# Queries of the third block: the bias added by products on TensorE, the constant factor moved out of the rounding chain

## What is computed

```python
def _L1_xattn_ref(x, cond, Wq, bq, Wkv, bkv, Wp, bp):
    ...
    q = (x @ Wq + bq).reshape(1, B * N, H, hd)
    ...
    scale = 1.0 / np.sqrt(hd).astype(np.float32)
    q = jnp.transpose(q * scale, (0, 2, 1, 3))
    ...
    q = _fq_sym(q, axis=-1)
    k = _fq_sym(k, axis=-1)
    ...
    attn = jnp.einsum('bhqd,bhkd->bhqk', q, k)
```

## Time and profile before

| | |
|---|---|
| median of 3 runs | 398.62 us (398.0 to 398.7) |
| span of the profiled execution | 396.3 us |
| PE busy | 301.0 us (76%) |
| DVE busy | 338.2 us (85%) |
| ACT busy | 316.7 us (80%) |
| POOL busy | 144.8 us (37%) |
| mean granted clock of PE | 0.926 |

### The profile page before, as it was taken

How to read it: one execution, slowest core, us unless ns; L and a number is a source line. 1 busy time by engine, 2 the same in 40 slices (tenths; PEclk the granted TensorE clock), 3 DMA queues, 4 the chain that set the end, 5 groups by cost and what they waited for, 6 DMA issues and landing times.

```text
span 396.3 us, 7494 instructions
## 1 busy us (share of the span) xinstructions
PE 301.0 (76%) x2589; PEld 186.2 (47%) x2589; DVE 338.2 (85%) x556; ACT 316.7 (80%) x517; POOL 144.8 (37%) x315
## 2 busy tenths in 40 slices
PE   7988999766796987567777857767576766884957
PEld 6755565322585874333444534444344343432434
DVE  4668999868889988778899998889999999678995
ACT  3785689967255789688999989899999999887771
POOL 6424524569500504004124565412222132247330
PEclk9989999899899999876899997999999999999576
DMA  8900023400200016569999988799899969800001
GB/s 268 388 5 3 0 74 96 203 2 0 106 0 2 2 29 124 107 99 173 163 168 175 177 158 132 140 185 174 151 156 166 156 130 148 136 1 2 26 31 50
DMA packets 126342, 42.68 MB, mean 108 GB/s; under 512 B 121056, under 2 KB 124768, under 8 KB 125536
## 3 DMA queue, kind: packets, MB, share of 16 engines
q1 hardware_dynamic: 125872, 41.60, 53.9%
q0 software_dynamic: 144, 0.52, 0.3%
q10 hardware_dynamic: 288, 0.07, 0.1%
HBM read 11.24 MB, written 1.05 MB: 31 GB/s over the span
## 4 chain that ended last, share of the span: by engine, by line
DVE 28%; PE 24%; ACT 23%; issue 16%; POOL 7%; DMA 1%; SPq 0%; ACTq 0%; DVEq 0%; POOLq 0%
ACT rb L973 15%; DVE nm L1452 5%; PE ps L1920 4%; PE ps L2015 4%; PE ps L1991 2%; DVE st L1108 2%; PE ps L2120 2%; PE ps L1785 1%; DVE ra L1557 1%; PE ps L2027 1%; DVE small L1559 1%; POOL ra L557 1%; POOL ra L558 1%; DMA xs<-x 1%; PE ps L1893 1%
## 5 line engine op out<-in xcount | busy, mean ns | idle before, releaser
L1452 DVE TENSOR_REDUCE nm<-ps 128x1 f32<-128x1024 f32 x128 | 153.1, 1217 | 12.6 <-PE ps L2015 11.6
L973 ACT ACTIVATE rb<-ps,eb,sq 128x1024 int16<-128x1024 f32 x128 | 153.7, 1214 | 11.8 <-POOL eb L639 11.1
L2015 PE MATMUL ps<-ra,rb 128*128 128x512 bf16 x256 | 82.8, 409 | 49.0 <-ACT rb L973 48.4
L639 POOL TENSOR_SCALAR eb<-nm,sq 128x1 f32<-128x1 f32 x128 | 34.2, 267 | 123.1 <-DVE nm L1452 122.1
L2015 PEld LDWEIGHTS ps<-ra,rb 128*128 128x128 bf16 x256 | 15.8, 99 | 67.7 <-ACT rb L973 63.9
L2042 PEld LDWEIGHTS ps<-ra,tern 128*128 128x128 f16 x624 | 26.0, 99 | 18.9 <-issue 9.2
L2042 PE MATMUL ps<-ra,tern 128*128 128x16 f16 x624 | 26.0, 171 | 2.6 <-DVE rb L1183 2.6
L973 ACT ACTIVATION_READ_ACCUMULATOR rb<-ps,eb,sq 128x1 f32 x128 | 27.0, 211 | 0.0
L1893 PE MATMUL ps<-xqT,tern 128*128 128x512 bf16 x64 | 17.2, 406 | 6.0 <-DVE rb L1361 4.9
L2027 PEld LDWEIGHTS ps<-idh,rb 128*128 128x128 f16 x224 | 14.3, 99 | 14.3 <-issue 7.7
L2027 PE MATMUL ps<-idh,rb 128*128 128x128 f16 x224 | 17.5, 222 | 4.6 <-issue 2.2
(11 more groups left out here) (240 smaller groups left out, 714.0 us busy)
## 6 DMA issues: line engine op xcount, KB each, us to landing
stage<-w SPq DMA_DIRECT2D x2, 1024.0 KB, 7.3
rb<-ra SPq DMA_DIRECT2D x16, 128.0 KB, 3.1
xs<-x SPq DMA_DIRECT2D x4, 256.0 KB, 4.5
cx<-ctx_in SPq DMA_DIRECT2D x4, 256.0 KB, 4.7
stage<-w_gate SPq DMA_DIRECT2D x1, 1024.0 KB, 7.7
stage<-w_up SPq DMA_DIRECT2D x1, 1024.0 KB, 10.6
stage<-w_down SPq DMA_DIRECT2D x1, 1024.0 KB, 4.8
cx<-wide_rows SPq DMA_DIRECT2D x1, 1024.0 KB, 7.9
```

What stands on the lines that cost most here:

```text
L639: nc.gpsimd.tensor_scalar(eb[:, u % 3:u % 3 + 1], nm[:, u % 3:u % 3 + 1], sq[:, t, h:h + 1], LN255, ALU.mult, ALU.add).then_inc(s_bias, 1)
L973: A(esc[u % E_RING], bank(2 * (u % 3), 2), ACT.Exp, bias=eb[:, u % 3:u % 3 + 1], scale=sq[:, t, h:h + 1], accum_out=es[:, t % 2, h:h + 1]) ...
L1452: V.tensor_reduce(nm[:, u % 3:u % 3 + 1], bank(2 * (u % 3), 2), AX.X, ALU.max, negate=True).then_inc(s_max, 1)
L2015: ins = M(bank(2 * (u % 3) + hf), qz[t % 2][:, h // 2, h % 2, :], kT[:, h // 2, 512 * hf:512 * hf + 512], start=True, stop=True)
```

## The change

The bias of the queries is added by a product on PE: `ones` (one row of 128) by `bq` (one row of 256) starts each sum in PSUM, and the two products of the projection add to it. DVE reads the sums from PSUM twice and writes no copy. The scale is made in two steps: `ks`, without the factor, from which the reciprocal is taken, and `sq`, which is `ks` times the factor; nothing on DVE waits for `sq`. The lower limit is divided by the factor.

```diff
-            def quantise_rows(psum, bias, factor, scale, out_i):
-
-
-                link(V.tensor_tensor(kb.rearrange("p (b n) -> p b n", b=2), psum.rearrange("p (b n) -> p b n", b=2),
-                                     bias.unsqueeze(1).to_broadcast([P, 2, D]), ALU.add))
-                kb3 = kb.rearrange("p (a d) -> p a d", d=HD)
-                link(V.tensor_reduce(ka[:, :], kb3, AX.X, ALU.max, apply_absolute_value=True))
-                link(V.tensor_scalar(scale, ka[:, :], factor / 127.0, QMIN, ALU.mult, ALU.max))
-                link(V.reciprocal(kr[:, :], scale))
-                if factor != 1.0:
-                    link(V.tensor_scalar(kr[:, :], kr[:, :], factor, None, ALU.mult))
-                return V.tensor_tensor(out_i.rearrange("p (a d) -> p a d", d=HD), kb3,
+            def quantise_rows(psum, factor, scale, out_i):
+
+
+                rows3 = psum.rearrange("p (a d) -> p a d", d=HD)
+                link(V.tensor_reduce(ka[:, :], rows3, AX.X, ALU.max, apply_absolute_value=True))
+                link(V.tensor_scalar(ks[:, :], ka[:, :], 1.0 / 127.0, QMIN / factor, ALU.mult, ALU.max))
+                V.tensor_scalar(scale, ks[:, :], factor, None, ALU.mult)
+                link(V.reciprocal(kr[:, :], ks[:, :]))
+                return V.tensor_tensor(out_i.rearrange("p (a d) -> p a d", d=HD), rows3,
                                        kr[:, :].unsqueeze(2).to_broadcast([P, 2 * H, HD]), ALU.mult)
...
-                quantise_rows(bank(Q_BANK), rowv["bq"], 0.25, sq[:, 2 * j:2 * j + 2, :].rearrange("p t h -> p (t h)"),
+                quantise_rows(bank(Q_BANK), 0.25, sq[:, 2 * j:2 * j + 2, :].rearrange("p t h -> p (t h)"),
                               ki).then_inc(q_int, 1)
...
                 for i in range(2):
                     t = 2 * j + i
+                    M(bank(Q_BANK)[:, D * i:D * i + D], ones[0:1, :], rowv["bq"][0:1, :], start=True, stop=False)
                     for k in range(2):
                         ins = M(bank(Q_BANK)[:, D * i:D * i + D], xn3T[:, k, P * t:P * t + P], wqs[:, k, :],
-                                start=(k == 0), stop=(k == 1))
+                                start=False, stop=(k == 1))
                 ins.then_inc(q_ps, 1)
```

## The result

| | median | runs | profiled execution: span, mean granted clock |
|---|---|---|---|
| before | 398.31 us | 397.97 to 398.7, 4 | 396.3 us, 0.926 |
| changed | 407.9 us | 405.86 to 409.27, 4 | 405.8 us, 0.870 |

The ratio is 1.0204, with a 95% interval of 1.0165 to 1.0244: slower, by some four times what was forecast (400.7 against 398.62 us, 0.5%). Medians are over all runs; ratios and intervals leave out runs more than 1.5% above the fastest of the same kernel, so a ratio can differ from that of the two medians. Two later comparisons of the same two programs gave 1.0139 (1.0093 to 1.0185) and 1.0179 (1.0120 to 1.0238).

The account below looks back on a forecast made before the run. No one engine bounds the whole; locally a PE and DVE chain does. Delay of +1.75 us after pairs 0 and 1 becomes +1.85, then +2.1: 396.3 + 2.1 = 398.4, plus 2.3 outside the span, 400.7 us; range 398.3 to 403.5.

Parts of the forecast that it names:

- What bounds: Third block's queries, 134 to 174 us: no one engine bounds; PE and DVE steps follow one another, late pairs without slack.
- DVE gives 0.8 us a pair: q_quant4 on DVE: bias add and factor multiplication leave the chain, saving 0.65 to 0.83 us a pair, 0.8 taken.
- dearer reading from PSUM: q_quant4 on DVE: by the skill's page two PSUM reads cost 0.13 us a pair, saving 0.67 instead of 0.8.
- PE pays 1.53 us a pair at full clock: Each q_project on PE: two one-row bias products lengthen it from 1.74 to 3.27 us, as in k_project.
- rival of the cheap bias: Each q_project: a bias product costs like any other, 0.87 us a projection instead of 1.53; 399.1 us, chance 0.08.
- Pairs 0 and 1, +1.75 us: First two query pairs: PE's delay less DVE's savings makes q_quant4(1) end and scores(4) start 1.75 us later.
- Pairs 2 and 3 cost almost nothing more: q_project(2) and (3): later starts move work out of the slow stretch; +1.85 after pair 2, +2.1 at attend(0).
- rival of the lasting low clock: q_project(2) and (3) wholly at 0.50, 6.4 us each: +4.15, then +2.5, together +6.7; 405.3 us, chance 0.10.
- The starting time: Whole kernel before the change: span 396.3 us, median of the runs 398.62 us, the 2.3 us between carried over.

Follow-up runs that it names:

- run 6: The changed kernel with the queries' bias product on all 128 rows (1/128 in the weights) instead of one row; 398.72 us, ratio 1.0008 to the kernel before.
- run 14: As run 6, but with the bias product on 32 of the 128 rows (1/32 in the weights); 406.38 us, ratio 1.0125 to the kernel before.
- run 5: The changed kernel without the bias products, the queries' bias left out of the computation; 397.29 us, ratio 0.9852 to the kernel before.

## Why the prediction was wrong

- *What bounds.* Right: the region is a chain of PE and DVE, and the rest kept its length (222.5 us against 223.1).
- *DVE gives 0.8 us a pair.* Right: 2.02 for 2.88 us in pairs 2 and 3, 0.86 less, a little more than the 0.83 at most that was forecast. The dearer reading from PSUM that the Trainium skill has (VectorE: DVE Perf Modes, on the TRN2 errata) is not in the trace: reduction and product took 0.69 us from PSUM.
- *PE pays 1.53 us a pair at full clock.* Right: 3.48 us from start to DVE's start, against 1.98, is 1.50, as in k_project. The rival of the cheap bias fell with it.
- *Pairs 0 and 1, +1.75 us.* Right: y_residual(5) started at 153.81, before at 148.05, 5.76 later; less the 4.10 that stood there already this is 1.66. DVE's wait for q_project(0) was 1.49 us (1.5 forecast), for q_project(1) 1.77, where "more than 2" was forecast.
- *Pairs 2 and 3 cost almost nothing more.* This is the step that failed, in the words "If the lower stretches fall where they fell": q_project(2) was to do the first 1.2 us at 0.50 and the rest at full clock. It ran at 0.50 from end to end, because the one-row products within it kept the clock from coming back, which run 6 undid by nothing but the row count (3.94 us instead of 6.41). The first maximum behind q_quant4(2) came at 171.40 against 163.33, less 4.10: +3.97, where the forecast had +1.85 and the rival of the lasting low clock +4.15. At q_quant4(3) it was +6.0, where the forecast had +2.1 and that rival +6.7; of the 0.7 between them 0.4 is scores(8), which the rival had put at the lower clock and which ran at full clock (0.62 us at 174.36). The rival's 6.4 us a projection were measured as 6.41, and it had got 0.10.
- *Why it got so little.* The reason given against it was that in the trace of before the clock came back right behind q_project(2). That was true of products on 128 rows, and I carried it to a mixture with one row. The trace of before held a warning that the prediction did not use: the fourth block's stretch from 368.5 us, with PE busy throughout and the clock still at 0.50 (shown behind run 14).
- *The starting time.* 396.3 us of span and runs within 0.7 us were taken as the kernel's time. The same program takes 396.3 to 405.5 us, with medians of 398.8 to 402.2, and the ends of that range go with the mean granted clock: 0.922 at 396.3 us, 0.902 at 405.55. Of the first 9.6 us of difference some 4 are this. The 5.6 to 7.2 us of the repeated comparisons are still some three times the forecast of +2.1, so the clock in pairs 2 and 3 is a miss of its own.

## What to carry to other kernels

A bias that is added by a product is not free on PE: give it all 128 rows (a constant 1/128, or 1/64 with an fp16 pair), which spared both the row switches and the clock here, and issue it where PE waits anyway, since it needs nothing but a free bank. Where a chain passes through PE behind a gap, price each step at both clock levels, and ask if the new form of work lets the clock come back. Before trusting a difference of 1%, time the unchanged kernel as its own rival: its spread is the yardstick.

## What was not expected of the hardware

- Products on 1 and on 32 rows, mixed with ones on 128, left the granted clock at 0.50 while PE was busy 6.6 of 6.6 us (run 14); with 128 rows it was back after 2.3 and 3.0 us of the two late projections (run 6).
- One pair of switches, 128 rows to one and back, costs 0.4 us at full clock: 3.48 against 3.08 us with half of them. Three profiles of one-row projections gave 6.41 or 6.42 us six times; projections of four products took 1.97 to 3.69 us in the profiles of before and of the factor alone.
- One small operation of DVE in q_quant4(0) took four times its time while POOL ran L575: L1177 0.72 us, where it takes 0.18 in the other pairs, as L1182 had once before. The rows of DVE and POOL in the changed kernel:

```profile
142.48 0.72 DVE L1177 TENSOR_SCALAR ks<-ka 128x32 f32<-128x32 f32 x1
```

```profile
141.88 1.27 POOL L575 TENSOR_TENSOR x<-xc,row 128x512 f32<-128x512 f32 x1
```

It ended as POOL's operation did (143.20 and 143.15), and so did the stretched operation of this pair in nine other profiles, among them run 6 (1.28 us from 139.57, POOL's 1.27 from 139.54). The reduction that reads PSUM, from 141.75, kept its 0.69 us although POOL's operation had begun. In run 5 no small operation of this pair met it, and its quantiser took 2.07 us. Only argued: that the two were in each other's way.
